# The third layer norm of a decoder layer is split into fp16 halves and turned by the DMA queue

## What is computed

```python
x = x + attn(layernorm(x))                  # a Toeplitz mixing over the row index
x = x + cross_attn(layernorm(x), ctx, ctx)  # causal softmax over 512 keys
x = x + ffn(layernorm(x))                   # 2 shared and 16 routed experts, the best 2 weighed
```

## Time and profile before

| | us |
|---|---|
| three runs of the kernel, median (lowest, highest) | 587.88 (586.95, 588.98) |
| the profiled execution, its span | 587.6 |
| TensorE busy in it | 556.6 |
| VectorE busy | 443.4 |
| ScalarE busy | 235.1 |
| GpSimd busy | 181.9 |

### The profile page before, as it was taken

One profiled execution on the slowest core, in us unless ns is written; L12 is line 12 of the kernel. 1 busy time (PEld: TensorE's weight loads), 2 busy tenths in 40 slices (PEclk: granted clock), 3 DMA queues, 4 the chain that ended last, 5 costly groups with the idle time before them and its releaser, 6 DMA issues. The chain is left out here.

```text
span 587.6 us, 13723 instructions
## 1 busy us (share of the span) xinstructions
PE 556.6 (95%) x5164; PEld 378.9 (64%) x5164; DVE 443.4 (75%) x1132; ACT 235.1 (40%) x463; POOL 181.9 (31%) x223
## 2 busy tenths in 40 slices
PE   6888889999999999999999999999999999999997
PEld 5566567566685666766686667666766666566455
DVE  5858688768975788868886898769876777677754
ACT  3555544443344243343344333342443323432332
POOL 4215150222532145123523333224421341223123
PEclk8979999999999999999999999999999999999999
DMA  8995595892439913595439831892269226400251
GB/s 251 291 362 191 182 387 171 183 348 99 109 79 230 343 34 89 122 268 178 108 76 241 258 107 54 176 345 79 67 135 301 77 78 123 87 2 1 72 111 37
DMA packets 90737, 94.75 MB, mean 161 GB/s; under 512 B 28224, under 2 KB 76224, under 8 KB 90432
## 3 DMA queue, kind: packets, MB, share of 16 engines
q1 hardware_dynamic: 90688, 94.09, 57.1%
HBM read 75.66 MB, written 12.12 MB: 149 GB/s over the span
## 5 line engine op out<-in xcount | busy, mean ns | idle before, releaser
L652 POOL TENSOR_TENSOR mid<-gated,mid 128x512 f16<-128x512 f32 x72 | 86.4, 1200 | 242.8 <-ACT mid L813 242.7
L813 ACT ACTIVATE mid<-gated 128x512 f16<-128x512 f32 x72 | 45.1, 626 | 108.5 <-DVEq L1123 108.5
L145 PE MATMUL wide<-w_d,mid 128*128 128x256 f16 x288 | 78.6, 273 | 0.0
L147 PE MATMUL wide<-w_d,mid 128*128 128x256 f16 x288 | 78.5, 273 | 0.0
L146 PE MATMUL wide<-w_d,mid 128*128 128x256 f16 x288 | 78.5, 273 | 0.0
L1104 DVE SCALAR_TENSOR_TENSOR gated<-gated,score 128x512 f32<-128x512 f32 x72 | 49.1, 682 | 36.4 <-ACT gated L808 35.2
L145 PE MATMUL score<-h3T,w_gu 128*128 128x512 f16 x160 | 60.7, 380 | 0.9 <-DVEq L125 0.8
L146 PE MATMUL rows<-h3T,w_gu 128*128 128x512 f16 x160 | 60.7, 380 | 0.0
L145 PE MATMUL rows<-h3T,w_gu 128*128 128x512 f16 x160 | 60.7, 380 | 0.0
L147 PE MATMUL score<-h3T,w_gu 128*128 128x512 f16 x160 | 60.7, 379 | 0.0
L146 PE MATMUL score<-h3T,w_gu 128*128 128x512 f16 x160 | 60.7, 379 | 0.0
(11 more groups left out here) (224 smaller groups left out, 1372.7 us busy)
## 6 DMA issues: line engine op xcount, KB each, us to landing
toep<-z_scratch SPq DMA_DIRECT2D x14, 2048.0 KB, 17.7
stage<-comb_scratch SPq DMA_DIRECT2D x32, 512.0 KB, 8.5
toep<-z_scratch SPq DMA_DIRECT2D x4, 1024.0 KB, 11.6
x_bo<-in_x SPq DMA_DIRECT2D x8, 512.0 KB, 11.6
x_in<-in_xr SPq DMA_DIRECT2D x7, 512.0 KB, 11.6
qT<-q_scratch SPq DMA_DIRECT2D x7, 512.0 KB, 3.9
vx<-v_scratch SPq DMA_DIRECT2D x7, 512.0 KB, 5.3
out<-x_out SPq DMA_DIRECT2D x7, 512.0 KB, 3.0
```

Of the source, the lines that this page charges most:

```text
L145: pe.matmul(out, stationary[0], moving[0], start=start, stop=False, **kw)
L147: return pe.matmul(out, stationary[1], moving[0], start=False, stop=stop, **kw)
L652: pool.tensor_tensor(mid_slot(j, 1, late), gate_slot(j, late), mid_slot(j, 0, late), ALU.subtract).then_inc(mid_split.sem, 1)
L813: act.activation(mid_slot(j, 0, late), gate_slot(j, late), ACT.Copy).then_inc(mid_hi.sem, 1)
```

## The change

ACT writes the high half of `h3` in row form, by halves of the rows, GpSimd subtracts to make the low half (in iterations 2 to 8 ACT's copies stand ahead of its `part_mid(7)` and behind its `tanh(8)`), and SP turns each half with one transposing transfer of 256 KB. The four planes lie in the space of `h2` (`h3_parts`). The eight transposes of TensorE, the two copies of ACT from PSUM and the two subtractions of DVE are gone for every batch. `h3T` gets the half of the rows as its outer dimension, so that `gate_up` reads two stretches of 256 columns. `logits` waits for the first transfer, and for the second ahead of its third block of rows. DVE no longer waits for the turning before it writes the next `h3`, but for GpSimd's split.

```diff
-        h3T = sb("h3T", [P, 2, K2, S], F16)
+        h3T = sb("h3T", [P, 2, 2, K2, S // 2], F16)
@@ sync
+            def move_h3(it, b, half, d):
+                if d:
+                    hold(sp, rows.ready, rows.is_ready(it, f"u{MID - 1}"))
+                else:
+                    sp.wait_ge(ctx_stored[1], 32)
+                hold(sp, h3_split, h3_split.at(b, half + 1))
+                sp.dma_start(h3T[:, half].rearrange("p a k (c s) -> p (a k c) s", s=P), h3_parts(half),
+                             transpose=True).then_inc(h3T_moved[half].sem, 16)
...
                 if f and m:
                     fetch_context(it, it)
                 if n and d:
                     move_h1(it + 1)
+                if m:
+                    for half in range(2):
+                        move_h3(it, it - 1, half, d)
@@ gpsimd
+            def part_h3(b, half):
+                pool.wait_ge(h3_hi.sem, h3_hi.at(b, half + 1))
+                pool.tensor_tensor(h3_rows(half, 1), h3[:, 2 * half:2 * half + 2].rearrange("p c (k e) -> p c k e", k=K2),
+                                   h3_rows(half, 0), ALU.subtract).then_inc(h3_split.sem, 1)
...
                 for j in range(MID):
+                    if d and m and j in (MID - 3, MID - 2):
+                        part_h3(it - 1, j - (MID - 3))
...
+                if first:
+                    for half in range(2):
+                        part_h3(it - 1, half)
@@ scalar
+            def part_h3(b, half):
+                act.wait_ge(h_ready[2].sem, h_ready[2].at(b, half + 1))
+                act.activation(h3_rows(half, 0), h3[:, 2 * half:2 * half + 2].rearrange("p c (k e) -> p c k e", k=K2),
+                               ACT.Copy).then_inc(h3_hi.sem, 1)
...
+                    if m and j == MID - 2:
+                        part_h3(it - 1, 0)
...
+                    if m and j == MID - 2:
+                        part_h3(it - 1, 1)
-                if d and m:
-                    act.wait_ge(rows.ready.sem, rows.is_ready(it, f"u{MID - 1}"))
-                if m:
-                    part_turned(it, it - 1, h3T, h3T_hi, "h3")
@@ tensor, logits
-                pe.wait_ge(turned.taken.sem, turned.is_taken(it - 1, "h3.1"))
                 for q in range(C):
+                    if q % 2 == 0:
+                        moved = h3T_moved[q // 2]
+                        pe.wait_ge(moved.sem, moved.at(it - 2, 16))
@@ tensor, iteration
-                    if d and m and j == MID - 1:
-                        gate_up(it, j, some=slice(0, 1))
-                        turn_halves(it, "h3", h3, h_ready[2], it - 1)
-                        gate_up(it, j, some=slice(1, 2))
-                    elif d:
+                    if d:
                         gate_up(it, j)
...
-                if m and not d:
-                    turn_halves(it, "h3", h3, h_ready[2], it - 1)
```

More of the change, by code:

```diff
@@ L53 @@
 X_MID = 16.0
-TURNED = ["mix.0", "mix.1", "combT", "h2.0", "h2.1", "pt0", "pt1", "p0", "pt2", "p1", "pt3", "p2", "p3", "h3.0", "h3.1",
-          "h1.0", "h1.1", "none"]
+TURNED = ["mix.0", "mix.1", "combT", "h2.0", "h2.1", "pt0", "pt1", "p0", "pt2", "p1", "pt3", "p2", "p3",
+          "none", "h1.0", "h1.1"]
 SCORE = ["z", "g0", "g1", "g2", "s0", "s1", "g3", "s2", "g4", "s3", "g5", "g6", "g7", "g8", "g9", "none"]
@@ L298, in decoder_layer @@
         cTs = [cT[:], w_q_k[:].rearrange("p w a k e -> p (w a k e)").rearrange("p (a k s) -> p a k s", a=2, k=K2)]
-        pairs = [(qT[:], vx[:]), (h3T[:], probT[:].rearrange("p a n (k e) -> p a (n k) e", e=E))]
+        h3T_flat = h3T[:].rearrange("p n a k s -> p (n a k s)")
+        pairs = [(qT[:], vx[:]), (h3T_flat.rearrange("p (a k s) -> p a k s", a=2, k=K2), probT[:].rearrange("p a n (k e) -> p a (n k) e", e=E))]
         for n in range(3):
@@ L363, in decoder_layer @@
         h2T_hi = sig("h2T_hi", 2)
-        h3T_hi = sig("h3T_hi", 2)
+        h3_hi = sig("h3_hi", 2)
+        h3_split = sig("h3_split", 2)
+        h3T_moved = [sig(f"h3T_moved{half}", 16) for half in range(2)]
         z_maxed = sig("z_maxed", 2)
@@ L435, in mid_slot, with h3_parts, h3_rows @@
             return mid[:, half, j % SLOTS]
+        def h3_parts(half):
+            at = 2 * K2 * 2 * P * half
+            return h2[:].rearrange("p c e -> p (c e)").bitcast(F16)[:, at:at + 2 * K2 * 2 * P]
+        def h3_rows(half, a):
+            return h3_parts(half).rearrange("p (a k c e) -> p a c k e", a=2, k=K2, c=2)[:, a]
         def context_unit(n, u, half):
@@ L1007, in normalise @@
             def normalise(b, it, n, src, dst, half=0):
-                if n and not half:
-                    dve.wait_ge(turned.ready.sem, turned.was_ready(it, f"h{n + 1}.1"))
+                if n == 1:
+                    dve.wait_ge(turned.ready.sem, turned.was_ready(it, "h2.1"))
+                elif n and not half and (not isinstance(b, int) or b > 0):
+                    dve.wait_ge(h3_split.sem, h3_split.at(b, 0))
                 dve.wait_ge(rstd_done[n].sem, rstd_done[n].at(b, half + 1))
@@ L1496, in logits @@
                 rows.fill(pe, it, "logit")
-                pe.wait_ge(turned.taken.sem, turned.is_taken(it - 1, "h3.1"))
                 for q in range(C):
+                    if q % 2 == 0:
+                        moved = h3T_moved[q // 2]
+                        pe.wait_ge(moved.sem, moved.at(it - 2, 16))
                     for k in range(K2):
                         last = three_passes(pe, rows.bank("logit")[:, NE * q:NE * q + NE],
-                                            parts(h3T, k, slice(P * q, P * q + P)), parts(w_r, k, slice(None)),
+                                            [h3T[:, q // 2, a, k, P * (q % 2):P * (q % 2) + P] for a in range(2)],
+                                            parts(w_r, k, slice(None)),
                                             start=(k == 0), stop=(k == K2 - 1))
@@ L1562, in gate_up @@
                     for k in range(K2):
-                        last = three_passes(pe, banks.bank(use)[:],
+                        last = three_passes(pe, banks.bank(use)[:].rearrange("p (n s) -> p n s", n=2),
                                             parts(w_gu, k, slice(2 * P * j + at, 2 * P * j + at + P)),
-                                            parts(h3T, k, slice(None)), start=(k == 0), stop=(k == K2 - 1))
+                                            [h3T[:, :, a, k] for a in range(2)], start=(k == 0), stop=(k == K2 - 1))
                     last.then_inc(banks.ready.sem, 1)
```

## The result

The changed kernel takes 603.31 us (median of 4 runs, 602.89 to 604.25), the kernel before on the same chip 588.07 (4 runs, 586.95 to 588.98). The ratio is 1.0254, 95% interval 1.0227 to 1.0280. The profiled execution took 602.89 us with a span of 601.1, against a span of 587.6 before: 13.5 us are in the two traces and can be found there. In the code after, the norm's L1013 is L1056, L1110 is L1153, L813 (ScalarE's half of the product) is L855 and L652 (GpSimd's) is L683. L677 is GpSimd's new subtraction, L499 SP's new pair of transposing transfers.

What follows compares the result with a forecast made beforehand. VectorE's chain with ScalarE and GpSimd, arriving at `down(9)` just ahead of TensorE, was taken as the bound. Stall 10.0, clock 2.0, collisions 1.8 and iteration 8 0.1 gave +13.9 on 587.9, about 602 us; range 594.5 to 609.

Steps and rivals of the forecast that it cites:

- What bounds the kernel: Two chains, TensorE and VectorE with ScalarE and GpSimd, reach `down(9)` within 0.35 us; it can move 0.25 us earlier per batch.
- Case D: Rival: VectorE is not the bound; `down(9)` moves the full 1.46 us in seven batches, -10.2 us, total 590; chance 0.05.
- The stall of iteration 1: First `logits` of iteration 2 waits for transposing transfers queued behind stores and loads: +10 us, between 8.5 and 11.5.
- Its signs: Would be wrong if first landing came before 97 us or iteration distance shrank over 1 us; distance expected within 0.5 us.
- case B: Rival: iteration 1's transposes run as soon as issued, the second landing at 97.4, a short stall; 595 us, chance 0.14.
- The clock: After TensorE's wait of over 10 us the granted clock drops to 0.50 for a stretch: +2.0 us, at most 3.1.
- GpSimd against VectorE: GpSimd's new subtractions collide with VectorE's norm and gate passes: +0.3 us in each of six batches, +1.8 us.
- case A: The forecast itself: stall, clock and small collisions, +0.3 us per batch; 597 to 606 us, chance 0.62.
- case C: Rival: GpSimd's two subtractions cost VectorE a full 0.8 us each, +1.3 us per batch; 608 us, chance 0.14.
- The slack: Steady iterations: `logits` may wait up to 0.8 us for its second half, at no cost while product 9 is later.
- Iterations 7 and 8: Iteration 8 has no `z` product between, so transfers and `down(9)` are due about 541.9: +0.1 us; nothing for iteration 7.
- Reads in two stretches: `gate_up` streaming 2 x 256 columns was costed at nothing.

Runs made afterwards that it cites:

- act_low: Changed kernel without GpSimd's two subtractions per batch; ScalarE writes zeros as the low half of `h3` instead: 600.15 us, ratio 1.0178.
- before_late8: Kernel before the change, with GpSimd's split of product 8 held until the pass of gate 9 is done: 583.98 us, ratio 0.9917.
- queue_first: Changed kernel with iteration 1's two transposing transfers issued ahead of context 5's stores and context 1's loads: 596.39 us, ratio 1.0126.
- wait_norm: Changed kernel with GpSimd's first subtraction of a batch held until VectorE has written the norm's second half: 599.17 us, ratio 1.0163.
- queue_z_gate: Changed kernel with iteration 1's transfers first, `z` ahead of `logits`, both subtractions behind product 7 and waiting for gate 8: 592.14 us, ratio 1.0066.
- queue_z_order: Changed kernel with iteration 1's transfers first, `z` ahead of `logits`, both subtractions behind product 7 without a wait for gate 8: 594.78 us, ratio 1.0111.
- queue_z_norm: Changed kernel with iteration 1's transfers first, iteration 2's `z` ahead of `logits`, GpSimd's first subtraction held for the norm: 589.21 us, ratio 1.0004.

## Why the prediction was right, and where it was not

The time (602 said, 603.31 measured) and the sign hold, and so does the place of the stall. That the sum came out so near is in part luck: two of its terms were too large and one far too small, and they made up for each other. In the spans, +13.9 were said; the stall has +8.15, the clock +1.0 and the batches +5.9, together 15.1, less the 1.56 of the first 45 us.

- **What bounds the kernel.** That VectorE's chain arrives at `down(9)` only just ahead of TensorE, so that less work on TensorE alone is worth next to nothing, is shown by `act_low`. With the transposes gone and GpSimd's load as before, the interval is 62.51, 0.35 less than before, and `down(9)` begins 0.06 us after product 9 is split. The forecast left 0.25 for this. Case D, with its 1.46 us per batch, falls. The converse is shown by `before_late8`: a hold on GpSimd, with TensorE's work untouched, brings 0.8%. It also shows something that the prediction did not see. It spoke of two chains side by side. But TensorE's 0.59 us ahead of `logits` are a wait for VectorE's subtraction of `h3T`, which stands behind the same pass of gate 9 as product 9. One collision held both chains, and one hold freed both.
- **The stall of iteration 1.** Right in place and releaser. Forecast +10.1 (91.47 to 101.6), measured 9.02 - 0.87 = 8.15. Two steps were off. From the end of the last load's issue to the end of `logits` it was 7.4 us (90.63 to 98.06) and not 8.5, for the load `vx` landed after 6.2 us instead of 7.7, without the slow rest of the earlier trace rows. And the forecast left the stores at 90.26, though they stand behind context 5, which TensorE reaches 0.87 us sooner without the transposes. That the transposes do not overtake stands: the loads landed by 95.64, the first transpose at 96.64, the second at 97.53.
- **Its signs.** The prediction was to be wrong if the first landing came before 97 us, and it came at 96.64. Counted from the end of the last load's issue, the second landed after 6.9 us, where the forecast had 8.1 and case B 4.3, and the head of this execution was 2.4 us shorter than before. So the sign was set too tightly, in absolute time, and case B is still not what happened. A second sign did fail: the distance between two iterations was to stay within 0.5 us of before, and moved by 0.91.
- **The clock.** Forecast +2.0, measured +1.0, from the last `logits` to the first `down` row. The stretches are these, in the columns of the earlier trace rows:

```profile
91.46:98.06 6.60, 0.96 (x25) 0.87 (x26) 0.00 (x0) 0.00 (x0) 0.00 (x0) 0.50 0.88 240
98.06:101.70 3.64, 3.64 (x13) 1.32 (x13) 2.40 (x18) 0.40 (x3) 0.00 (x0) 0.50 0.02 7
```

The clock is at its level of 1.2 GHz for 10.24 us, but 6.60 of them lie in the wait and in `logits`. Only 3.64 us of full work behind `logits` fall into it, where the shorter wait of the earlier trace rows was followed by 6.11. The loss of the clock alone was not tried by itself. In `queue_first`, with a wait of 2.1 us, the clock was at 0.50 from 91.8 to 95.2, all of it under work, and the same stretch was 26.0 us long, against 26.2 in the changed kernel and 25.2 before: the shorter wait saved hardly anything of this term.

- **GpSimd against VectorE.** This is the term that failed: forecast +1.8 for six batches and +0.1 for the eighth iteration, measured 0.97 + 4.96 = +5.9 for iterations 2 to 8, of which +1.21 in iteration 7 is matched by the transfers alone. The failing sentence is "Its first block runs; its second meets GpSimd and ends at about 349.95". The forecast had GpSimd begin at 348.5 and the norm at 348.48, and took this order of 0.02 us for granted. In the run the order was the other way, by 0.01 us: the first block met the subtraction and the second met product 7 behind it. The norm was put at 1.5 us and took 2.46. The other two collisions came out as mild as forecast or milder: the pass of gate 8 took its 0.69 us, that of gate 9 its 1.54 as before. With 1.28 us per batch in place of 0.55 the same working gives 0.93 less the slack that it used, and 0.91 is there. Net of the slack that lies between case A's 0.3 and case C's 1.3 per batch, nearer to C. The Trainium skill (SBUF - State Buffer, the section on the two separate sides of SBUF) says that whoever starts first has the shared ports for its whole instruction and the other blocks. The trace agrees: both blocks ended 0.14 to 0.15 us after the GpSimd instruction that had begun before them.
- **The slack.** "It costs nothing so long as product 9 is later" holds for the transfers of iterations 2 to 6. But a new wait was missed: TensorE, ahead by the transposes that are gone, now meets the `z` product's bank before gate 9 has read it, 1.54 us. It costs nothing of its own, since product 9 is later still.
- **Iterations 7 and 8.** With no `z` product between, `logits` waits 0.43 and 0.71 us in iteration 7 and 0.47 and 0.70 us in iteration 8 for the transfers; the forecast had nothing in the seventh and +0.1 in the eighth. The second lands 4.8 us after `u9` is done (489.29 to 494.06), so `down(9)` begins 5.1 us after `u9`, where it was 3.8 before; and `u9` of iteration 7 is done only 0.1 us sooner, not 0.87.
- **Reads in two stretches** at nothing: nothing speaks against it, since `wait_norm` with these reads has shorter batches than the kernel before.

What stays open: `act_low`, `wait_norm`, `queue_z_gate` and `queue_z_order` are 2 to 5 us above what their intervals in the loop let one expect. Part of it lies in iteration 7 (the transfers, in every kernel that has them), part in stretches at the lower clock, whose number differs between executions of one kernel: of the ten of `queue_z_norm`, the four with a mean granted clock of 0.997 took 586.8 to 588.8 us and the five at 0.991 or less 589.7 to 592.8. A wait of 1.1 to 1.6 us for `mixT` near 500 us, in some profiled executions and not in others, is a third part. No run separates them or says what brings them on. And no kernel was run in which the transposes are moved and neither product 7 nor the transfers of iteration 7 wait, so what the moved transposes could bring at best is not known.

## What to carry to other kernels

Moving work off the busiest engine brings nothing while another chain reaches the same instruction within a few tenths; look for who arrives last there before pricing the work that goes, and ask whether the busiest engine's own waits hang on that chain too. Where GpSimd and VectorE both work from SBUF to SBUF, the start time of GpSimd's instruction matters more than its length, and hundredths of a microsecond decide who waits: a hold of 0.8 to 1.0 us, which costs no work, was worth 0.6 to 1.4 us in each batch of the loop. But a hold pushes back what stands behind it on GpSimd's queue, and that becomes the next wait. And a transfer placed in a strict queue is as late as what the queue waits for ahead of it, and then as the bytes ahead of it; give it its place by when it is needed.

## What the runs showed of the hardware beyond that

- Two VectorE blocks behind one another (L1056) each lost to the GpSimd instruction that had begun 0.01 and 0.11 us before it: 2.46 us for a pair that takes 0.74. The multiplication L1153, in the same position against one instruction, took 1.54 to 1.66.
- It goes both ways. GpSimd's subtraction of 1.16 us took 1.59 when it began 0.12 us behind VectorE's multiplication (361.89 and 361.77, above).
- After 9.1 us without work, TensorE's clock was back at full speed after 4.6 us of work, 3.64 of them behind `logits`. After the 2.0 us of the earlier trace rows it took 6.11 us. The longer wait was not the dearer one, since its slow stretch began inside it.
- The first 45 us of one and the same program part ran at a mean granted clock of 0.89 to 1.00 in different executions. Between the kernel before and after this went with 1.6 us, as much as many changes are worth. Compare from a common point in the trace, and leave such a head to the medians.
